# Blank rows of the pair table: twelve transfers on GpSimd's queue, or 182 rows with each tile on SyncE's queue

## The reference

```python
x = x + ssm(layernorm(x))            # layer 0: selective state space, 8 heads of 64, state 128
x = x + xattn(layernorm(x), ctx)     # 16 heads of 16, rotary
x = x + lstm_like(layernorm(x))      # a recurrence over the 64 sequences
x = x + gqa(layernorm(x))            # layer 1: grouped-query attention
x = x + xattn2(layernorm(x), ctx)    # one head of 256
x = x + moe(layernorm(x))            # 8 experts, each token goes to the best 2, plus a shared one

# in moe:
scores = sigmoid(xf @ gate_w.T + lb_bias)
topw, topi = top_k(scores, 2)
for e in range(8):
    m = topi == e
    wmean = (topw * m).sum() / m.sum()
    out += where(m.any(-1), mlp_e(xf) * wmean, 0)
out += shared_mlp(xf)
```

## Time and profile before

| | |
|---|---|
| median of three runs | 3533.28 us |
| the profiled execution, its span | 3528.69 us, 3526.9 us |
| mean granted TensorE clock | 0.951 of full speed |
| TensorE busy | 3097.6 us (88%) |
| VectorE busy | 2780.0 us (79%) |
| ScalarE busy | 2267.1 us (64%) |
| GpSimd busy | 1532.2 us (43%) |
| moved by DMA | 162.13 MB, mean 46 GB/s |

### The profile page before, as it was taken

One profiled execution on the slowest core, in us unless ns is written; L12 is line 12 of the kernel. 1 busy time (PEld: TensorE's weight loads), 2 busy tenths in 40 slices (PEclk: granted clock), 3 DMA queues, 4 the chain that ended last, 5 costly groups with the idle time before them and its releaser, 6 DMA issues. The chain is left out here.

```text
span 3526.9 us, 95395 instructions
## 1 busy us (share of the span) xinstructions
PE 3097.6 (88%) x27092; PEld 2670.7 (76%) x27093; DVE 2780.0 (79%) x8725; ACT 2267.1 (64%) x8246; POOL 1532.2 (43%) x5125
## 2 busy tenths in 40 slices
PE   6149999999999999999998689999999999399998
PEld 4047888888888888888887577777777777287998
DVE  5148888888888888888886478888888887488776
ACT  4026777777777777777776477777777777033333
POOL 1124445444444444544443145555555554033333
PEclk9569999999999999999999799999999999599999
DMA  6930000100100000000010100000000000022443
GB/s 181 218 84 28 32 27 28 34 27 27 36 27 27 33 30 27 30 33 27 27 36 14 59 18 16 18 18 15 18 18 18 15 18 14 2 88 109 136 139 91
DMA packets 92223, 162.13 MB, mean 46 GB/s; under 512 B 13379, under 2 KB 57776, under 8 KB 92144
## 3 DMA queue, kind: packets, MB, share of 16 engines
q1 hardware_dynamic: 73616, 102.32, 9.8%
q0 software_dynamic: 18528, 58.84, 5.7%
HBM read 102.85 MB, written 61.79 MB: 47 GB/s over the span
## 5 line engine op out<-in xcount | busy, mean ns | idle before, releaser
L386 POOL TENSOR_TENSOR tiny<-tiny 128x1 f32<-128x1 f32 x3456 | 779.6, 226 | 801.1 <-DVE tiny L373 560.4
L803 ACT ACTIVATE work<-bank,att 128x128 f32<-128x128 f32 x2048 | 722.2, 378 | 57.2 <-DVE att L793 51.2
L803 ACT ACTIVATION_READ_ACCUMULATOR work<-bank,att 128x1 f32 x2048 | 445.3, 217 | 0.0
L793 DVE TENSOR_REDUCE att<-bank 128x4 f32<-128x512 f32 x512 | 334.2, 684 | 45.6 <-PE bank L786 45.6
L822 PE MATMUL bank<-const,work 128*128 128x128 f32 x2048 | 317.1, 278 | 22.3 <-ACT work L803 18.2
L786 PEld LDWEIGHTS bank<-work 32*128 32x128 f32 x4096 | 253.7, 189 | 107.0 <-issue 74.6
L1268 DVE SCALAR_TENSOR_TENSOR work<-work,small 128x127 f32<-128x127 f32 (+2 forms) x1152 | 318.7, 345 | 9.9 <-ACT work L1108 5.2
L786 PE MATMUL bank<-work 32*128 32x128 f32 x4096 | 302.4, 286 | 20.1 <-ACT work L1153 2.5
L386 POOL TENSOR_TENSOR tiny<-tiny,const 128x1 f32<-128x1 f32 x1152 | 248.2, 215 | 90.2
L822 PEld LDWEIGHTS bank<-const,work 128*128 128x128 f32 x2048 | 238.6, 142 | 61.9 <-ACT work L803 38.7
L186 PE MATMUL bank<-w1r,workr 128*128 (+2 forms) x802 | 267.8, 334 | 0.4 <-issue 0.2
(11 more groups left out here) (357 smaller groups left out, 8486.2 us busy)
## 6 DMA issues: line engine op xcount, KB each, us to landing
work<-decay_sums SPq DMA_DIRECT2D x64, 512.0 KB, 3.6
pair_rows<-extra POOLq DMA_DIRECT2D x8, 2944.0 KB, 27.8
work<-pair_rows SPq DMA_DIRECT2D x91, 258.0 KB, 2.8
work<-in_ctx SPq DMA_DIRECT2D x128, 128.0 KB, 2.0
x_res<-in_x POOLq DMA_DIRECT2D x8, 1024.0 KB, 17.5
recurrence_out<-r_xo_ SPq DMA_DIRECT2D x64, 128.0 KB, 1.7
work<-recurrence_out SPq DMA_DIRECT2D x64, 128.0 KB
out_dram<-work POOLq DMA_INDIRECT x91
```

The costliest lines, as they stand in the source:

```text
L386: e.tensor_tensor(out_, a_, b_, ALU.add if b_ is three_halves else ALU.mult)\
L793: e.tensor_reduce(a_nm[:, 4 * g:4 * g + 4], sc_banks[g % 2][:, :].rearrange("p (h k) -> p h k", k=P), AX.X, ALU.max, negate=True).then_inc ...
L803: last = e.activation(Pb[g % 2][:, c * P:c * P + P], sc_banks[g % 2][:, c * P:c * P + P], ACT.Exp, bias=a_nm[:, 4 * g + c:4 * g + c + 1], ...
```

## The change

The twelve transfers on GpSimd's queue go, with the wait before them and the wait for their landing at the end of GpSimd's block. The memsets and the iota that make `blank` and `blank_end` stay. The table shrinks from 92 to 91 groups of 128 rows, 11648 rows, which is 182 for each of the 64 tiles. SyncE's program gets a function `blank_rows(b)` that writes 182 rows with three transfers (91 partitions with two rows each: twice 256 floats a row, once 4), behind `load_context` in each step, in the loop too. SyncE waits for `blank_ready` before its first step, and for the landing of all 192 transfers at its end.

```diff
-BLANKS = 4 * -(-SLOTS // 4)
...
-        slots = nc.dram_tensor("pair_rows", (BLANKS * P, ROW), F32, kind="Internal").ap()
+        slots = nc.dram_tensor("pair_rows", (SLOTS * P, ROW), F32, kind="Internal").ap()
...
+                def blank_rows(b):
+
+                    n = SLOTS * P // NB
+                    rows_b = slots[0:NB * n].rearrange("(b p s) d -> b p s d", b=NB, p=n // 2)
+                    rows_b = rows_b[b] if isinstance(b, int) else rows_b[ds(b, 1)].rearrange("o p s d -> p (o s) d")
+                    for at, n_, of in ((0, D, blank), (D, D, blank), (2 * D, 4, blank_end)):
+                        e.dma_start(rows_b[:, :, at:at + n_], of[0:n // 2].unsqueeze(1).to_broadcast([n // 2, 2, n_]))\
+                            .then_inc(S["blank"], 16)
...
                     b = i
                     if live(b):
                         load_context(b)
-
+                    b = i
+                    if live(b):
+                        blank_rows(b)
+
+                e.wait_ge(S["blank_ready"], 2)
                 pipeline(e, 4, step)
                 e.wait_ge(S["r_store"], 16 * NB)
+                e.wait_ge(S["blank"], 3 * 16 * NB)
...
-                e.wait_ge(S["blank_ready"], 2)
-                for k in range(4):
-                    rows_k = slots.rearrange("(s k p) d -> k p s d", k=4, p=P)[k]
-                    for at, n, of in ((0, D, blank), (D, D, blank), (2 * D, 4, blank_end)):
-                        e.dma_start(rows_k[:, :, at:at + n], of.unsqueeze(1).to_broadcast([P, BLANKS // 4, n]))\
-                            .then_inc(S["blank"], 16)
...
                 pipeline(e, 5, step)
-                e.wait_ge(S["blank"], 12 * 16)
```

## The result

The changed kernel takes 3442.5 us (median of four runs, 3439.0 to 3445.6) where the kernel before takes 3533.0 (median of four too, one more than the prediction had): a ratio of 0.975, with a 95% interval of 0.9728 to 0.9772. The forecast was 3441. The profiled execution took 3439.03 us, its span is 3437.2 us, 89.7 less than before.

A forecast was written before the change was run, and what follows sets the result against it. Bound: at layer 0's head, compute idles while twelve transfers hold GpSimd; in the loop, VectorE and TensorE. 3528.7 - 89.8 + 0 = 3438.9, or 3443.5 from the median; predicted 3441 us, forecast range 3428 to 3450, 8 of 10 within 3428 to 3478.

The forecast's parts named there:

- The head: Start of layer 0: scale_tokens starts 87.3 us earlier, and earlier decay sums of tile 1 bring 2.5 us; 89.8 us removed.
- The wait behind the hole: After the idle stretch at layer 0's head: VectorE's 9.04 us wait for decay_sums is gone or under 1.
- SyncE's issue time: Loop, SyncE's queue: three more issues a turn, 0.33 to 0.47 us each, delay the next sums by 0 to 0.3 us.
- the upper bound of 1.8: Loop, SyncE's queue: at 0.99 us an issue, as when the DMA engines were full, sums are 1.8 us late.
- three blanks and sums inside 2.6 us: Sign in the later profile: a loop turn on SyncE's queue shows context, three blanks and sums within 2.6 us.
- waits for `decay_sums` stay near nothing: Sign in the later profile: in the loop VectorE hardly waits for the sums, with turns 26.7 us apart.
- The DMA engines' term: Loop: a tile's blanks take 1.62 us of DMA time; delay to the sums taken as none to 0.5 us.
- DMA share in the loop: Sign in the later profile: the DMA engines' share of the loop goes from 0.09 to about 0.15.
- The slack: Loop: sums can land 1.16 us later, plus 0.76 us from line 1330's wait for GpSimd, 1.92 us in all.
- The sums come late in each turn: Rival, loop: sums 2.5 us late stall 0.6 us a turn, 35 us; 3476, span 3450 to 3510; chance 0.21.
- Slower through the queue: Rival, loop: blanks drained before sums; over 3.4 us late decides, 4.4 us late gives 3589; chance 0.06.

The follow-up runs named there:

- big_on_sync: Changed kernel with the small transfers replaced by the former twelve large ones, all issued on SyncE behind the first context load: 3523.1 us, ratio 0.9996 to the kernel before.
- one_wide: Changed kernel with one transfer of 182 rows of 516 floats a tile instead of three, at the same place: 3434.7 us, ratio 0.9712 to the kernel before.
- behind_sums: Changed kernel with the blanks issued right behind the load of decay sums instead of behind the context load: 3431.4 us, ratio 0.9734 to the kernel before.
- rows192: Changed kernel with a table of 96 groups, so 192 rows a tile from 96 partitions, same place: 3436.7 us, ratio 0.9742 to the kernel before.
- twice: Changed kernel with each tile's blanks written again into a second, unread table, at the same place: 3692.6 us, ratio 1.0468 to the kernel before.

## Why the prediction was right, point by point

**The head (87.3 + 2.5 us) was right.** The forecast of 89.8 stands against 90.4, both at line 1281 and at the first context load of the loop. The reasoning that mattered was to ask at which time the input of `scale_tokens` was ready, and what would be late next. One reading was too narrow: the full queue of GpSimd was named as the cause, and big_on_sync shows that a hole of the same length arises from SyncE's queue. It is 24 MB issued at once ahead of something needed soon, and whichever engine issues them stands still.

**The wait behind the hole** was forecast gone or under 1 us and is 2.24. It costs nothing, as line 1281 waits for ScalarE until later anyway.

**SyncE's issue time was mis-sized.** The step took 0.33 to 0.47 us an issue from rows of 128 partitions and got 0 to 0.3 us of delay. Measured are 0.9 us and 4.21 - 2.31 = 1.9 us of delay, just over the upper bound of 1.8. So the text's "three blanks and sums inside 2.6 us" and "waits for `decay_sums` stay near nothing" did not come true (4.21 us, and 53 us of waits). The bound was near for another reason than its own: it came from issues of 0.99 us while the DMA engines were full, and in the loop they were not.

**The DMA engines' term came out right, in part by luck:** 0.1 us of delay (3.7 against 3.6) where none to 0.5 was taken. But this is the delay with issues of 0.9 us instead of 0.33 to 0.47; in one_wide, where the blanks' bytes come closer together, it was 1.3 us. DMA share in the loop 0.14, forecast about 0.15.

**The slack was right, and it carried the result.** 1.16 + 0.76 = 1.92 us were read from two waits, against 1.9 + 0.1 = 2.0 us of delay. What is left over, 0.08 us a turn, is the measured 26.78 - 26.70, though so exact a match is chance: the changed kernel's second trace has 26.84, and behind_sums has 26.73 without any wait. The other runs bear the slack out better. With the sums issued 0.95 us later than before (rows192) VectorE waited 2.1 us in all; with 1.3 us (one_wide, by the landing) it waited 20.1 us and the turn was no longer; with 2.0 us the turn grew by 0.08; with 4.9 us (twice) by 4.4. Had there been only the first 1.16 us of slack, a delay of 2.0 us would have cost 0.84 x 58 = 49 us, and with none at all 2.0 x 58 = 116 us. Thanks to the slack the error in the issue time cost 4 to 5 us.

**That the sum hit to 1.5 us is luck.** The spread of the changed kernel's runs alone is 6.6 us. In the profiled pair, the head gave 0.6 us more than forecast, the loop cost 4.2 where nothing was forecast, and 3.5 us came from the end of layer 0 and from layer 1, where nothing was forecast either; they happen to cancel.

**The rivals.** "The sums come late in each turn" is what happened in kind, at 0.08 us a turn instead of 0.6. "Slower through the queue" needed the sums 3.4 us late; twice issued them 4.9 us late and ended 4.7% slower than the kernel before, so such a point exists; the changed kernel's 2.0 us stayed 1.4 us short of the 3.4. But the delay in twice came from SyncE's issues, not from the blanks' time in the DMA engines, on which the rival rested: with the blanks doubled the sums still landed in 3.7 us.

## What to carry to other kernels

A large transfer that nobody needs soon belongs in small pieces into a queue that has room, and into that place of the turn behind which its engine waits longest, or in so few issues that the next load goes out on time. What a late load costs is read from the chain of waits behind it: its own slack, and the next wait that it would eat. The time of an issue is taken from a row with the same shape, or it is bounded by the dearest row.

## What the runs showed of the hardware that I had not expected

An issue on SyncE took 0.33 us for 128 rows, 0.59 for 192 rows from 96 partitions and 0.90 for 182 rows from 91, and for the last two shapes it was the same within 0.03 us for 16 bytes, 1024 or 2064 bytes a row. In big_on_sync, with 24 MB issued at once, the transfers of 16 bytes a row held SyncE longer than those of 1024 bytes with 64 times the data, in ns:

```profile
L904 SPq DMA_DIRECT2D pair_rows<-extra x8: 427/7490/11064, 93.2 to 181.2; - x8
L904 SPq DMA_DIRECT2D pair_rows<-work x4: 11187/11326/11599, 100.5 to 187.7; - x4
```

This is not the price of the narrow rows themselves. While SyncE was held at the last of them (187 to 199.3 us), the DMA engines moved 287 GB/s, some 3.5 MB, and a narrow transfer has only 46 KB in all: they were writing the wide rows issued before it. So the length of such an issue tells what lies ahead of it, not what it carries. For the narrow rows there is the prediction's estimate from DMA shares, 7.75 us for 2944 of them.

And a late load can cost more than its delay: in twice, TensorE idle for 2.88 us was followed by 2.9 us at half its clock, which made four matmuls 1.2 us slower.
